# An attention pair with a mixture of experts on one core: a new prologue, routing work reordered, split last out-projections, and shared and routed expert pairs two units later

## The chip, the cores and the metric

One core of a Trainium2 chip runs the whole program. Its engines work side by side and are tied together by semaphores only: TensorE (PE; its weight loads are listed as PEld), VectorE (DVE), ScalarE (ACT), GpSimd (POOL), and the DMA queues, most of them fed by SyncE (SP), some by ACT and POOL. Each engine carries out its own list of instructions in order. The metric is the time of one execution on the device in microseconds (us).

## What is computed

The input x is 2 sequences of 512 tokens with 256 features, float32. All the rest is float32 too.

```python
x = L0_attn_x
xn = _layernorm(x, axis=-1)
x = x + _L0_attn_ref(xn, ...) + _L0_ffn_ref(xn, ...)
return x
```

`_L0_attn_ref` is causal attention with 16 heads of 128, biases on queries, keys, values and output. `_L0_ffn_ref` is a whole transformer block:

```python
x = rmsnorm(hidden_states, ln1_w)
q = (x @ wq) ...; k = (x @ wk) ...; v = (x @ wv) ...   # 16 query heads, 4 key/value heads
q = q * cos + rotate_half(q) * sin                      # k alike
attn = softmax(causal(q k^T / sqrt(D)))
x = resid + (attn v) @ wo
xn = rmsnorm(x, ln2_w)
probs = softmax(xn @ gate_w.T)                          # 32 experts
_, sel = top_k(probs + bias_e, 4)
rw = probs[sel]; rw = rw / max(sum(rw), 1e-12)
moe_y = sum over the 4 chosen experts of rw * ((silu(xn @ weg) * (xn @ weu)) @ wed)
shared = silu(xn @ wsg) * (xn @ wsu) @ wsd
return x + moe_y + shared
```

## The kernel before

The work is cut into 64 units of one head and one sequence each: units 0 to 31 (`HALF`) are the heads of the rotary attention inside the block, units 32 to 63 those of the plain attention. Every engine runs `step(n)` for n from -2 to 63 (`windows`, line 425), and in step n it works on several units at once: PE makes the scores of unit n+1, turns the probabilities of unit n, multiplies them with the values (`attend`), projects queries, keys and values of unit n+2 (`project`), and does half an output projection of an earlier pair of heads (`out_project`). The probabilities go around all engines: scores on PE, mask and row maximum on DVE (L1368), exponential on ACT (L1103), reciprocal of the sum on DVE (L1374), scaling on POOL (L675), transposes on PE (L955), and a split into a rounded part (ACT, L1118) and a rest (DVE, L1383). Matrix products of float32 data are made of three passes over such parts (`mm3`, L820). Below, "step n" is the stretch from the first scores product of unit n+1 (L940) to that of unit n+2.

What stands in `step` is written out by hand, and so is the order of the projections' results in the four PSUM banks j0, j1, zb and ob (`ring_of`, `CHUNK`, `BANK`). A bank is filled again only when the engine that empties it has said so (`kept`, `vacant`).

The prologue loads x (L443), then biases and norm weights, then the first weights, all on the SP queue. DVE takes mean and variance of each token tile of 128 (`bn_stats`, L1319), POOL raises to the power -1/2 (`power`, L602), DVE writes the normalised rows xn (L1329), ACT squares and sums them (L1081), DVE and POOL make the second factor, and DVE writes the rows xr of the inner root-mean-square norm (L1338). PE transposes xr and xn (`turn_xr`, `turn_xn`, L801), ACT and DVE split the result (L1094, L1354, L1092, L1352). POOL splits the weights (`weights`, L661 and L665). `b_O` is added on POOL in steps 1 and 2 (L767).

Between steps 34 and 40 the routing is done beside the attention: squares (SQUARED), rows scaled (SCALED), transposes T2, the logits L in step 36 (`LOGITS`, L874), then DVE's long list `route_0` to `route_3`: softmax, the four best of 32 (L1670, L1744), combine weights `cw` (L1725, L1755), ranks by a triangular product R in step 38 (`RANKS`, L881, L883), slot numbers (L1731), the match of slots and experts over 128x1024 elements (L1765, L1685, L1700). In the plain half, `route_1` stands before the queries and keys of the step are taken out of PSUM (`chunk`), `route_2` between them and the values' product `z_part`. POOL scatters the rows into `x_slots` in HBM (L686, 32 transfers, `SENT`: steps 40 to 43), SP then loads them in slots (L540) and loads the weights of the experts (L528, L531).

Four shared pairs of token tiles follow, one a step, in steps 40 to 43 (`DENSE` = HALF + 8), and 32 pairs of expert blocks, two a step, in steps 44 to 59 (`MOE` = HALF + 12): PE transposes X (L890), makes gate and up G (L902, L909) and down Y (L917). POOL adds the result to one of two sums in HBM by a scatter with addition (L711), in the step after. When both sums are complete, SP loads each in one transfer of 1 MB (L571), DVE adds those of the second sequence in step 63 (L1710), POOL those of the first (L781), DVE adds the last out-projections of steps 64 and 65 (L1470), and SP stores four pairs of tiles in order (L579).

The lines around the last steps on PE:

```python
windows(pe, step)
for n in (UNITS, UNITS + 1):
    out_project(n, 0, None)
    out_project(n, 1, None)
```

## Time and profile before

| | |
|---|---|
| median of 3 runs | 793.09 us (790.8 to 795.21) |
| the profiled execution's own time | 791.5 us |
| its span (first to last instruction) | 789.7 us |
| busy PE / DVE / ACT / POOL | 738.3 / 548.8 / 490.2 / 477.8 us |
| PE's share in the chain that ended last | 64% |
| mean granted clock of TensorE | 0.988 |
| read from and written to HBM | 51.75 MB, 24.82 MB |

The page gives each engine's busy time, then the span in 40 slices (a digit is the busy share in tenths; PEclk is TensorE's granted clock). A timeline row is: start, duration, engine, line, operation, output<-inputs, count, and in brackets the idle time of the engine before it with what ended it. Ends of matmuls are modelled, so a busy PE says less than the start of the next group.

### The profile page before, as it was taken

The numbers are of one execution on the slowest core, as the hardware profiler recorded it, in microseconds if no ns is written. First come the engines' busy times: TensorE is split into PE (matmuls) and PEld (weight loads), VectorE is DVE, ScalarE is ACT, GpSimd is POOL, SyncE is SP. The second block draws the span as 40 slices with busy tenths as digits, with TensorE's granted clock in tenths as the row PEclk, the third lists the DMA queues.
The fourth block names the chain that finished last, engine by engine and source line by source line (L and its number), as shares of the span: only waits on it lengthen the run. The fifth ranks groups of instructions, "written<-read, shape, count | busy, mean of one in ns | idle before, by whom it ended". The sixth has DMA issues, their size and how long they took to land.

```text
span 789.7 us, 14401 instructions
## 1 busy us (share of the span) xinstructions
PE 738.3 (93%) x4629; PEld 661.2 (84%) x4629; DVE 548.8 (69%) x1689; ACT 490.2 (62%) x1230; POOL 477.8 (60%) x552
## 2 busy tenths in 40 slices
PE   1899999999999999999988995999999999999995
PEld 1678888888888888989877885999999999999995
DVE  5878888797878887675788763555555655555575
ACT  3777768777777775666434662556655566555652
POOL 3679676776867684327223774566556675665543
PEclk9999999999999999999999997999999999999999
DMA  5000000100010099201000534566797677776351
GB/s 170 27 15 28 14 15 15 34 15 21 24 45 28 14 308 295 73 14 42 14 28 14 184 110 130 128 142 157 165 266 159 162 163 162 176 173 142 68 133 54
DMA packets 103491, 77.51 MB, mean 98 GB/s; under 512 B 6950, under 2 KB 102266, under 8 KB 103418
## 3 DMA queue, kind: packets, MB, share of 16 engines
q1 hardware_dynamic: 92234, 63.19, 28.1%
q0 software_dynamic: 10752, 12.74, 9.7%
q8 instruction: 38, 0.62, 0.4%
q10 hardware_dynamic: 432, 0.67, 0.3%
q14 instruction: 35, 0.29, 0.1%
HBM read 51.75 MB, written 24.82 MB: 97 GB/s over the span
## 4 chain that ended last, share of the span: by engine, by line
PE 64%; DVE 13%; ACT 9%; POOL 7%; issue 4%; DMA 2%; DVEq 0%; SPq 0%; POOLq 0%; ACTq 0%
PE j L820 17%; PE zb L820 8%; PE ob L820 8%; PE s L820 8%; PE t L955 6%; ACT probs L1103 4%; POOL x_slots_dram L686 4%; PE j L909 4%; DVE probsT L1383 3%; PE zb L909 2%; PE ob L909 2%; PE j L917 2%; ACT rope_swapped L1143 2%; ACT rope_swapped L1144 2%; DVE rope_sum L1415 1%
## 5 line engine op out<-in xcount | busy, mean ns | idle before, releaser
L675 POOL TENSOR_SCALAR probs<-probs,inv_sum 128x128 f32<-128x128 f32 x244 | 141.8, 592 | 166.9 <-DVE inv_sum L1374 162.9
L1103 ACT ACTIVATE probs<-probs,neg_max 128x128 f32<-128x128 f32 (+3 forms) x256 | 143.1, 560 | 126.4 <-DVE neg_max L1368 124.9
L820 PE MATMUL s<-k_heads,q_heads 128*128 128x256 f32 (+2 forms) x576 | 138.1, 360 | 3.4 <-DVE neg_max L1368 2.8
L1368 DVE CUSTOM_DVE_ANT_0 probs<-s,mask 128x128 f32<-128x128 f32 (+3 forms) x256 | 119.9, 484 | 11.7 <-PE s L820 6.6
L711 POOL DMA_INDIRECT moe_sum_dram<-late,slot_tokens x64 | 101.4, 1584 | 38.7 <-ACT late L1188 25.7
L1383 DVE TENSOR_TENSOR probsT<-t,probsT 128x384 fp32r<-128x384 f32 (+2 forms) x192 | 101.1, 547 | 12.7 <-ACT probsT L1118 11.9
L1118 ACT ACTIVATE probsT<-t 128x384 fp32r<-128x384 f32 (+2 forms) x192 | 89.8, 486 | 19.4 <-PE t L955 19.3
L955 PE MATMUL t<-ident,probs 128*128 128x128 f32 x640 | 94.3, 274 | 7.8 <-POOL probs L675 6.5
L820 PEld LDWEIGHTS s<-k_heads,q_heads 128*128 128x128 f32 x576 | 90.9, 189 | 10.2 <-DVE neg_max L1368 6.6
L955 PEld LDWEIGHTS t<-ident,probs 128*128 128x128 f32 x640 | 74.9, 140 | 16.6 <-POOL probs L675 8.6
L820 PE MATMUL zb<-probsT,v_heads 128*128 128x512 f32 (+2 forms) x351 | 68.3, 339 | 1.4 <-DVE probsT L1383 0.9
L820 PEld LDWEIGHTS zb<-probsT,v_heads 128*128 128x128 f32 x351 | 60.1, 189 | 8.2 <-DVE probsT L1383 1.4
L720 POOL TENSOR_TENSOR rope_swapped<-rope_swapped,rope 128x512 f32<-128x512 f32 x32 | 41.4, 1295 | 34.1 <-ACT rope_swapped L1144 34.1
L1374 DVE RECIPROCAL inv_sum<-row_sum 128x1 f32<-128x1 f32 x256 | 36.0, 156 | 34.0 <-ACT probs L1103 33.8
L820 PE MATMUL ob<-w_o,zT 128*128 128x256 f32 x420 | 58.4, 283 | 0.0
L820 PEld LDWEIGHTS ob<-w_o,zT 128*128 128x128 f32 x420 | 55.5, 190 | 2.6
L820 PE MATMUL j<-xrT,w_qk 128*128 128x512 f32 x192 | 53.1, 412 | 0.8 <-DVE rope_sum L1415 0.7
L1103 ACT ACTIVATION_READ_ACCUMULATOR probs<-probs,neg_max 128x1 f32 x256 | 47.9, 187 | 0.0
L726 POOL TENSOR_TENSOR q_heads<-rope_sum,q_heads 128x384 fp32r<-128x384 f32 x32 | 38.8, 1212 | 12.5 <-ACT q_heads L1211 10.7
L820 PE MATMUL j<-xnT,w_qk 128*128 128x512 f32 x174 | 45.5, 404 | 0.0
L820 PEld LDWEIGHTS j<-xrT,w_qk 128*128 128x128 f32 x192 | 34.3, 192 | 7.7 <-DVE rope_sum L1415 1.1
L820 PEld LDWEIGHTS j<-xnT,w_qk 128*128 128x128 f32 x174 | 32.8, 193 | 6.8
(251 smaller groups left out, 1576.9 us busy)
## 6 DMA issues: line engine op xcount, KB each, us to landing
x_slots_dram<-mask SPq DMA_DIRECT2D x1, 8480.0 KB, 38.3
late<-x_slots_dram SPq DMA_DIRECT2D x32, 265.0 KB, 4.5
late<-in_L_ffn_weg_dram SPq DMA_DIRECT2D x64, 128.0 KB
late<-in_L_ffn_weu_dram SPq DMA_DIRECT2D x64, 128.0 KB
late<-in_L_ffn_wed_dram SPq DMA_DIRECT2D x64, 128.0 KB
moe_sum_dram<-mask SPq DMA_DIRECT2D x2, 1152.0 KB, 8.8
raw_qk<-in_L_ffn_wq_dram SPq DMA_DIRECT2D x16, 128.0 KB, 2.2
raw_o<-in_L_ffn_wo_dram SPq DMA_DIRECT2D x8, 256.0 KB, 2.6
```

The lines of the kernel that those rows point to most:

```text
L675: pool.tensor_scalar(piece, piece, rinv[:, u % 2, i:i + 1], 1.0, ALU.mult, ALU.mult).then_inc(p_norm, 1)
L711: pool.indirect_dma_start(out=moe_sum[j][:, :], out_offset=bass.IndirectOffsetOnAxis(ap=ids[:, r % 4, j:j + 1], axis=0), in_=yb[:, r % 2, ...
L720: pool.tensor_tensor(swapped[kind], swapped[kind], sinT, ALU.mult).then_inc(rp_sin[kind], 1)
L726: pool.tensor_tensor(qT[:, v % 2, 1], rot_sum((kind, v))[:, P:S], qT[:, v % 2, 0].bitcast(f32), ALU.subtract).then_inc(rp_lo[kind], 1)
L820: m = pe.matmul(dst, lhs(a), rhs(b), start=first and i == 0, stop=last_ and i == 2, skip_group_check=skip)
L909: m = pe.matmul(dst[:, (2 * w + j) * P:(2 * w + j + 1) * P], wgu[(r - SHARED) % 3][:, j, k, w * P:(w + 1) * P], xbT[:, r % 2, k, j * P:(j ...
L955: m = pe.transpose(bT[at % 2][:, (j - lo_) * P:(j - lo_ + 1) * P], pr[:, u % 2, P_OFF[qt] + kt * P:P_OFF[qt] + (kt + 1) * P], ident[:, :])
L1103: act.activation(piece, piece, ACT.Exp, bias=nmax[:, u % 2, i:i + 1], scale=-1.0, accum_out=rsum[:, u % 2, i:i + 1]).then_inc(e_done, 1)
L1118: act.activation(pT[:, 0, (first - 1) * P:(b - 1) * P], bT[(3 * u + c) % 2][:, (first - a) * P:(b - a) * P], ACT.Copy).then_inc(pt_hi, 1)
L1368: ve.tensor_tensor_reduce(pr[:, u % 2, P_OFF[i]:P_OFF[i] + width], bS[i % 2][:, 0:width], mask_t[:, S - width:S], INV_SCALE, BIG, ALU.add, ...
L1374: ve.reciprocal(rinv[:, u % 2, i:i + 1], rsum[:, u % 2, i:i + 1]).then_inc(r_done, 1)
L1383: ve.tensor_tensor(pT[:, 1, cs], bT[(3 * u + c) % 2][:, (first - a) * P:(b - a) * P], pT[:, 0, cs].bitcast(f32), ALU.subtract).then_inc(pt ...
```

## The change

The program computes the same result. What it does:

- **Prologue.** xr is made straight from x with one factor, (var (1 + 1e-6) + 1e-11)^-0.5, which holds both norms; the squares and the first pass of xn fall away. Rows of the second sequence are made on POOL (`second_rows`). x of the second sequence is loaded behind the first weights; the small rows go on ACT's queue, ahead of the rotary table. ACT loads its table by an exponential of its own. PE makes six products into an unused bank (`keep_busy`).
- **xn** is written by POOL in steps 0, 1, 4 and 5 and transposed in a new chunk `XN` at the start of the step behind each; `b_O` is added in steps 9 and 17.
- **Rotary steps.** The values `Vx` are taken out of PSUM by DVE later in the step, and the last mask of the step comes before the probabilities' rest.
- **Routing.** `route_1` and `route_2` stand behind queries, keys and z. `cw` is gone: weights are normalised after the match, over 4 values. POOL makes the triangle and the ones (step 36) and the product of match and probabilities (`choice`, step 39).
- **Pairs.** DENSE = HALF + 10 and MOE = HALF + 14: shared pairs in steps 42 to 45, expert pairs in steps 46 to 61.
- **End.** The last out-projections are split by head; PE adds the experts' sums of the second sequence by products with the identity (`add_experts`) in place of DVE; SP loads the sums in four transfers, the second sequence first. Step 63's out-projection moves into step 62.

```diff
-    DENSE, MOE = HALF + 8, HALF + 12
+    DENSE, MOE = HALF + 10, HALF + 14
...
-    ACT_NORMS = (HALF + 9, HALF + 10, HALF + 11)
+    ACT_NORMS = (HALF + 8, HALF + 9, HALF + 10, HALF + 11)
...
-            for j in range(2):
-                sp.wait_ge(y_out[j], 16 * (PAIRS - SHARED))
-                sp.dma_start(macc[j], moe_sum[j][P:P + B * S, :].rearrange("(t p) d -> p t d", p=P)).then_inc(acc_in, 16)
+            for b in reversed(range(B)):
+                for j in range(2):
+                    sp.wait_ge(y_out[j], 16 * (PAIRS - SHARED))
+                    sp.dma_start(macc[j][:, b * TB:(b + 1) * TB, :],
+                                 moe_sum[j][P + b * S:P + (b + 1) * S, :].rearrange("(t p) d -> p t d", p=P)
+                                 ).then_inc(acc_in[b], 16)
...
+            def choice(n):
+
+                if n == RANKS + 1:
+                    pool.wait_ge(chosen_done, 1)
+                    pool.tensor_tensor(match, match, route[:, 0, :, 0:E].unsqueeze(2).to_broadcast([P, NT, TOPK, E]),
+                                       ALU.mult).then_inc(weighed, 1)
...
-                    if n == -2 and job[0] == "Q2":
+                    if n == -2 and job[0] == "Q3":
+                        first_powers(1)
                         q_sin(n, it)
+                        second_rows(range(TB, TB + 2))
                         q_lo(n, it)
+                        second_rows(range(TB + 2, NT))
                     weights(job, it)
+                choice(n)
...
-                if n in (1, 2):
+                    normal_power()
+                normal_rows(n)
+                if n in (GS + 1, 2 * GS + 1):
                     pool.wait_ge(bc_in, 32)
+                    pool.wait_ge(normal, NT)
...
+            def keep_busy(count):
+
+                for _ in range(count):
+                    pe.matmul(bT[0][:, :], ident[:, :], mask_t[:, :], start=True, stop=True)
...
+            def add_experts(n):
+
+                o = n - 2
+                half, b = o % 2, o % GS // 4
+                pe.wait_ge(acc_in[b], 32)
+                for t in range(2):
+                    for j in range(2):
+                        pe.matmul(bR[BANK["O", n]][:, t * D:(t + 1) * D], ident[:, :], macc[j][:, b * TB + 2 * half + t, :],
+                                  start=False, stop=False, skip_group_check=True)
...
+            def last_unit():
+
+                for t in range(2):
+                    out_project(UNITS, t, None, (0,))
+                turn_probs(UNITS - 1, 2, None)
+                for t in range(2):
+                    out_project(UNITS + 1, t, None, (0,))
+                attend(UNITS - 1, None)
+                for n in (UNITS, UNITS + 1):
+                    add_experts(n)
+                for n in (UNITS, UNITS + 1):
+                    for t in range(2):
+                        out_project(n, t, None, (1,))
...
+                did(ve.tensor_scalar(var[:, 1, ts], mv[:, ts, 1], 1.0 + 1e-06, 1e-11, ALU.mult, ALU.add), "var", b)
...
                 v_last = behind(n, 1, "Vx")
-                for ch in v_last:
-                    chunk(ch, it)
...
+                if v_last:
+                    mask_scores(n + 1, 3, it)
                 probs_lo(n, 2, it)
-                mask_scores(n + 1, 3, it)
+                if not v_last:
+                    mask_scores(n + 1, 3, it)
...
                 rope_sum(chs[0], it)
+                for ch in v_last:
+                    chunk(ch, it)
...
+                    for ch in chs[:2]:
+                        chunk(ch, it)
+                    z_part(n, it)
                     route_1(n)
-                    for ch in chs[:1]:
-                        chunk(ch, it)
-                    for ch in chs[1:2]:
-                        chunk(ch, it)
                     route_2(n)
-                    z_part(n, it)
...
                 if n == RANKS + 2:
-                    then(ve.tensor_tensor(match, match, cw.unsqueeze(2).to_broadcast([P, NT, TOPK, E]), ALU.mult))
+                    ve.wait_ge(weighed, 1)
+                    then(ve.tensor_reduce(x2r[:, :, D + 1 + TOPK:ROW], match, AX.X, ALU.add))
+                    then(ve.tensor_reduce(rsm[:, 3], x2r[:, :, D + 1 + TOPK:ROW], AX.X, ALU.add))
+                    then(ve.tensor_scalar(rsm[:, 0], rsm[:, 3], 1e-12, None, ALU.max))
+                    then(ve.reciprocal(rsm[:, 1], rsm[:, 0]))
+                    ve.tensor_tensor(x2r[:, :, D + 1 + TOPK:ROW], x2r[:, :, D + 1 + TOPK:ROW],
+                                     rsm[:, 1].unsqueeze(2).to_broadcast([P, NT, TOPK]), ALU.mult).then_inc(rows_done, 1)
```

## Rows read from the trace of the kernel before

**Rows 1.** Timeline of the prologue, from the first statistics to unit 1's scores.

```profile
5.97 1.40 DVE L1319 BATCH_NORM_STATS2 ln_stats<-acc_b 128x6 f32<-128x256 f32 x4 [5.97 <-DMA acc_b<-in_L_attn_x_dram]
...
8.01 1.04 POOL L602 TENSOR_TENSOR rstd<-var,minus_half 128x4 f32<-128x4 f32 x1 [5.48 <-DVE var L1325]
...
15.37 1.14 DVE L1338 TENSOR_SCALAR probs<-acc_a,rstd 128x256 f32<-128x256 f32 x4 [1.13 <-POOL rstd L602]
...
18.84 2.90 PE L820 MATMUL j<-xrT,w_kv 128*128 128x512 f32 x6 [0.94 <-DVE xrT L1354]
...
24.12 1.54 PE L820 MATMUL j<-xrT,w_kv 128*128 128x512 f32 x6
...
37.32 0.39 PE L940 MATMUL s<-k_first,rope_sum 128*128 128x128 f32 x2
```

**Rows 2.** Timeline: PE's wait for unit 1's first mask.

```profile
39.54 1.50 PE L820 MATMUL s<-k_heads,q_heads 128*128 128x384 f32 x6 [1.25 <-DVE neg_max L1368]
```

**Rows 3.** Timeline: b_O's second addition; PE's wait in step 7.

```profile
65.86 2.40 POOL L767 TENSOR_TENSOR acc_b<-acc_b,b_o 128x1024 f32<-128x1024 f32 x1
...
106.90 1.09 PE L955 MATMUL t<-ident,probs 128*128 128x128 f32 x8 [0.53 <-POOL probs L675]
```

**Rows 4.** Timeline of step 38: `cw` on DVE beside POOL's split, ranks on PE.

```profile
393.15 1.33 POOL L665 TENSOR_TENSOR w_qk<-raw_qk,w_qk 128x512 fp32r<-128x512 f32 x1
...
393.37 1.39 DVE L1725 TENSOR_TENSOR combine<-router 128x256 f32<-128x256 f32 x1
...
397.35 0.67 PE L881 MATMUL ob<-router,late 128*128 128x256 f32 x2 [2.10 <-DVE late L1750]
```

**Rows 5.** Timeline of step 40: waits, a shared pair's products, DVE's reduction.

```profile
421.17 0.46 PE L940 MATMUL s<-k_first,q_first 128*128 128x128 f32 x2 [1.10 <-DVE k_heads L1422]
...
425.98 0.79 PE L820 MATMUL s<-k_heads,q_heads 128*128 128x384 f32 x3 [0.97 <-DVE neg_max L1368]
...
426.61 1.89 PE L902 MATMUL ob<-late 128*128 128x256 f32 x8
...
432.10 1.20 DVE L1700 TENSOR_REDUCE late<-late 128x32 f32<-128x1024 f32 x1
```

**Rows 6.** Windows by step: length, busy us, clock, DMA share, GB/s.

```profile
363.07:380.97 17.90, 17.90 (x104) 16.09 (x103) 9.03 (x27) 8.25 (x22) 7.40 (x8) 0.81 0.16 44
421.17:435.56 14.39, 13.33 (x75) 11.52 (x75) 12.63 (x41) 5.76 (x16) 3.00 (x5) 1.00 0.08 19
474.07:501.44 27.37, 18.59 (x113) 16.68 (x112) 9.97 (x33) 10.15 (x25) 11.66 (x13) 0.81 0.31 94
501.44:517.89 16.45, 16.45 (x113) 15.08 (x111) 9.77 (x32) 9.87 (x26) 10.40 (x11) 1.00 0.70 162
748.20:758.43 10.23, 10.23 (x64) 9.25 (x63) 6.36 (x21) 6.21 (x17) 8.21 (x8) 1.00 0.44 63
...
767.49:789.70 22.21, 13.91 (x95) 12.14 (x93) 14.08 (x31) 6.36 (x17) 7.61 (x8) 0.97 0.14 48
```

**Rows 7.** Timeline: last row scattered, first transpose of an expert pair.

```profile
478.14 0.96 POOL L686 DMA_INDIRECT x_slots_dram<-late,dest  x1 [0.30 <-issue]
...
483.60 1.09 PE L890 MATMUL j<-ident,late 128*128 128x128 f32 x4 [8.78 <-DMA late<-x_slots_dram]
```

**Rows 8.** Timeline of the end: last scatter of a sum, last additions.

```profile
756.07 1.58 POOL L711 DMA_INDIRECT moe_sum_dram<-late,slot_tokens  x1 [0.16 <-issue]
...
774.89 5.59 POOL L781 TENSOR_TENSOR acc_b<-acc_b,late 128x512 f32<-128x512 f32 x4
...
786.44 0.69 DVE L1470 TENSOR_TENSOR acc_b<-ob,acc_b 128x512 f32<-128x512 f32 x1 [0.74 <-PE ob L820]
```

**Rows 9.** DMA view: KB of one, median us to landing.

```profile
late<-moe_sum_dram SPq DMA_DIRECT2D x2, 1024.0 KB, 5.7
...
moe_sum_dram<-late,slot_tokens POOLq DMA_INDIRECT x64, 5.1
out_dram<-acc_b SPq DMA_DIRECT2D x4, 256.0 KB, 2.1
```

More of the change, by code:

```diff
@@ L57, in attention_pair_moe_kernel @@
     BIG = 3.0e38
+    XN_UNITS = (0, 1, 4, 5)
     def chunks_of(n):
@@ L484, in _ @@
             kinds = ("KV", "Q0", "Q1", "Q2", "Q3", "O0", "O1")
-            for which in kinds:
+            load("KV", 0, 0)
+            sp.dma_start(accB[:, TB:2 * TB, :], xv[:, TB:2 * TB, :]).then_inc(x_in[1], 16)
+            for which in kinds[1:]:
                 load(which, 0, 0)
@@ L610, in _ @@
             pool.wait_ge(consts, 3)
-            for b in range(B):
-                power(0, b)
+            first_powers(0)
             def weights(job, it):
@@ L770, in _ @@
             weights(("KV", 0), None)
-            for b in range(B):
-                power(1, b)
             pool.wait_ge(rope_in, 16)
             windows(pool, step)
-            pool.wait_ge(acc_in, 32)
+            pool.wait_ge(acc_in[0], 32)
             kept(pool, ("O", UNITS - GS + 5))
```

272 lines of the change are left out of this document (138 added, 134 removed).

## The prediction

> **What bounds the kernel now.** I read the page first: PE is busy for 93% of the span and heads the chain that ended last, so what counts is where PE stands still or runs at half clock, and what is added to it. Next came the view of who waited for whom, for PE alone. Its largest entries are the start, where PE has nothing to do until constants and xr are there, and one wait of 8.78 us for the first expert rows [rows 7]; the rest are dozens of small ones. Then the windows, cut at each step's first scores product, and the timeline where a step is longer than its like. A plain step of the second half lasts 10.23 us with PE never idle, one with two expert pairs 16.45 [rows 6]. The surplus lies in four places, and the change touches all four: the prologue, 37.32 us long [rows 1]; the routing steps 36 to 40; step 44, 27.37 us instead of 16.45; and the end, 22.21 us from the start of step 62 [rows 6].
>
> **Prologue.** Before, the power for the first sequence is done at 8.01 + 1.04 = 9.05, and xr starts at 15.37 [rows 1], after xn, the squares and a second power. The new factor needs the first power only: 6.3 us go, less some 0.5 for four rows with two operations in place of one. x of the first sequence is in at 5.97, beside a rotary table and a second half of x; both now come later. A transfer of 512 KB lies between the rows for 256 KB (2.1 us) and 1024 KB (5.7 us) [rows 9], about 3.3 us by line, so up to 1.9 us are free; bounds 0 to 1.9, I take 1.3. The first six 512-column products take 2.90 us and a later group 1.54 [rows 1]: half clock and full. The six products of `keep_busy` fill PE's idle time before them; gain 0 (clock not granted in time) to 1.4, or a loss of about 1 if they are still running when xr is there. I take 0.8, since PE had nothing before that and works nearly without pause now. Rows of the second sequence move to POOL, ahead of the third and fourth query weights; its queue then holds power, sine product, two rows, query rest, two rows. By the old distances this lands where the old order did, seven small operations against two splits moved ahead. The xn transposes and four pairs of evictions leave the stretch, worth 2 us of PE, ACT and DVE before unit 1's scores. Sum: 6.3 - 0.5 + 1.3 + 0.8 + 2.0 = 9.9 us, bounds 6 to 12.
>
> **Rotary steps.** Unit 1's first mask waited for xn on DVE, 1.25 us at PE [rows 2]: -1.1. The xn work comes back as four chunks of four transposes (0.45 us), an ACT copy and a DVE rest of 0.7 us each, in steps 1, 2, 5 and 6, where PE is full: +0.6 each, +2.4. In step 5 the chunk shares bank ob with an out-projection that comes early on PE, which must wait for DVE: +0.7. The two b_O additions take 2.40 us of POOL each [rows 3]; before, the second stands ahead of the sine product of step 3, on which queries and scaling wait; of its length POOL could have hidden about 1 us, so 1.4 are on the path. In steps 9 and 17 POOL has more room, since no new keys or values are worked on beside it: 0 to 0.7 each, I take 0.3. Net -0.8. The later `Vx` brings the step's last mask, exponential and scaling 0.6 us forward; PE waits 0.53 us for that scaling in step 7 [rows 3] and in six more of the kind. Gain 0 to 0.53 each, I take 0.43: -3.0. Sum: -1.1 + 2.4 + 0.7 - 0.8 - 3.0 = -1.8.
>
> **Routing.** The key wait of 1.10 us in step 39 [rows 5] goes, with the ranks' wait of 2.10 [rows 4], since triangle and ones are POOL's by then and DVE's cw work (1.39 us [rows 4] and small instructions behind it) is gone. Following DVE's list through, I get steps 36 and 37 together unchanged (z no longer has routing work in its own wait), step 38 2.2 us and step 39 1.2 us shorter. Step 40 gives it back. There DVE now waits for POOL's product over 128x1024 elements, 2.40 us by the b_O row of that size [rows 3], where DVE did it itself in about the 1.20 that its reduction of that size takes [rows 5]. The product starts when DVE's match is done, and DVE has under 2 us of work to hide it. That reduction and four small ones stood later in the step, and now stand at once behind the wait. Queued behind them: the values' eviction, two reciprocals, the accumulation, and the masks of unit 41's last two tiles, on which its probabilities and PE wait. I count 3 us from match to the end of the wait and 2.1 for the sums, so step 40 takes about 15.6 us although the shared pair, 2.6 us, has left it: 14.39 - 2.6 = 11.8 [rows 6], +3.8. Sum: -2.2 - 1.2 + 3.8 = +0.4, bounds -3 to +3.
>
> In this trace DVE's product for cw took 1.39 us while POOL's split ran from 393.15 for 1.33 us, and ended when that ended [rows 4]. The Trainium skill (SBUF — State Buffer, "Who interferes with whom") has the rule: DVE and GpSimd share a pair of ports, and an instruction of DVE with two SBUF inputs, or in a two-port mode, is blocked for the whole length of a GpSimd instruction that has the pair. That rule speaks against this change. By it the small instructions behind the match could wait for POOL's product, and step 40 would be some 1.5 us longer.
>
> **Pairs two units later.** The last of 32 rows is scattered at 478.14 and PE gets its first expert rows at 483.60 [rows 8]. With MOE at step 46, two plain steps of 10.23 us stand before the four shared ones, and DVE hands over the rows some 7 us sooner, so the first X comes over 12 us after its rows. POOL needs 32 x 1.26 us for them (0.96 and 0.30 idle [rows 7]) and starts in step 40. The wait goes, and with it the half clock behind it (granted 0.81 in that step): 27.37 - 16.45 = 10.9 us [rows 6]. The two plain steps and the two pair steps trade places, which costs PE nothing. Gain 10.9, bounds 8 to 11.
>
> **End.** Before, the last scatter is issued at 756.07 [rows 8], two steps ahead, and the sums are in SBUF long before they are needed. Now the last scatter falls into step 62, by step 60's pattern 756.07 - 748.20 = 7.9 us after its start. It lands some 4.7 later, a little under the median of 5.1 [rows 9], as less runs beside it: 12.6. Then 0.5 MB for the second sequence is still to load, 3.3 us: 15.9, and 1 MB more for the first, 4.7 us by the slope (5.7 - 2.1) / 768 KB: 20.6. PE's part: eight float32 products of 256 columns; four of a shared pair are listed with 1.89 us, modelled end included [rows 5], so 3.1 to 3.8. With 1.5 for the second heads, 0.7 for an accumulation [rows 8] and 2.1 for a store [rows 9]: 24. POOL's part: four additions, 5.59 us with DVE beside them [rows 8], 5.2 alone: 25.8, then stores issued in order behind it: 29.2. The end was at 22.21 [rows 6]; +7.0, bounds +2 (both waits short) to +11 (a landing 1.5 us later and loads half as long again). What the split out-projections save DVE and PE, 2 us, is hidden behind this.
>
> **Sum.** -9.9 - 1.8 + 0.4 - 10.9 + 7.0 = -15.2 us against the profiled execution, 791.5 us: 776.3. That execution lies 1.6 us under the median of 793.09, so the median comes to 778; I say 777.
>
> One thing stays open: in step 36 the clock is 0.81 [rows 6], which is 17.90 x 0.19 = 3.4 us of PE lost; the small logits products stand just before the fall. It may come at another time or not at all; I keep it, and put 3.4 us in the bounds.
>
> **Rivals.** (A) The forecast, 777: 0.60. (B) The end hides better: PE takes the experts' rows at once and POOL's loads overlap, so the end grows by 2 us, and the clock stays up in step 36: 777 - 5 - 3.4 = 769. For it: sums of 1 MB loaded in 5.7 us before with nothing beside; against it: four POOL additions in a row. 0.17. (C) The prologue gains only the 6 us of the removed detour, and DVE's small instructions in step 40 end only with POOL's product, as DVE's did with POOL's in [rows 4], its 2.4 us and some wait behind: 777 + 3.9 + 3 = 784. 0.15. This is the result that the rule cited above would give. (D) The change doesn't do what it says, the wait for the first expert rows only moves, because POOL scatters later: 777 + 10.9 = 788. Against it: 32 x 1.26 = 40 us from step 40's beginning end before step 44 begins. 0.05. (E) Slower than before: in steps 40 and 41, now without shared pairs and with 5 us of waits, PE falls to half clock (1.2 GHz) and stays there for both plain steps, 2 x 10.23 = 20.5 us more: 777 + 20.5 = 797.5. It decides from the point at which waits in step 40 stretch so far that the granted clock falls, and it costs more than the whole gain only if it holds beyond one and a half steps. Against it: the fall in step 44 came after 8.78 us without work and was over within that step [rows 6, 7]. 0.03.
>
> **Numbers.** The range has to hold A with its bounds, most of B and of C: 766 to 787. A measurement of this kernel can tell about 0.5% (4 us) from no change: faster than 789.1 holds A, B, C but for their edges: 0.91; within 0.5%, to 797.1, D: 0.06; slower, E: 0.03.
>
> **What would show it.** Unit 1's scores at 27.4 us instead of 37.32; the first six 512-column products in under 2 us; no wait at the transposes of step 7 and its like; the ranks' products without wait; in step 40 a DVE wait on POOL and PE idle for 4 to 5 us; no wait at the first X, no half clock near it, and the X rows loaded 12 us ahead; in the end PE's first identity product about 16 us and POOL's first addition about 20.6 us after step 62's start, the last store 29. Wrong would be: a prologue held by const rows that come late on ACT's queue, an end that is hidden, or a fall of the clock in a place where there was none.

## The result, and the profile after

The changed kernel takes 804.2 us (median of 4 runs, 803.08 to 808.48), the kernel before 793.65 beside it. The two medians stand 1.3% apart; the ratio on record is 1.016, 95% interval 1.0135 to 1.0185. The change made the kernel slower. The forecast was 777 us, with 766 to 787 as its range. Its profiled execution has a span of 801.3 us against 789.7: 11.6 us more, where the forecast had 15.2 less.

Cut at the same marks as before (the first scores product of a unit, L996 now), the span divides as follows. The sum of the last column is the 11.6 us.

| stretch | before, us | after, us | difference | forecast |
|---|---|---|---|---|
| start to unit 1's scores | 37.32 | 31.76 | -5.6 | -9.9 |
| steps 0 to 7 | 71.91 | 93.77 | **+21.9** | -1.8 for steps 0 to 27 |
| steps 8 to 27 | 174.64 | 173.43 | -1.2 | |
| steps 28 to 35 | 79.21 | 79.18 | 0.0 | 0 |
| steps 36 to 40 | 72.49 | 69.86 | -2.6 | -2.2, since a shared pair of 2.6 moves out |
| steps 41 to 61 | 331.93 | 324.14 | -7.8 | -8.3, with that pair back |
| step 62 to the end | 22.20 | 29.14 | +6.9 | +7.0 |

The forecast and the two spans differ by 26.8 us. Steps 0 to 27 make 22.5 of them, nearly all in the first eight steps, and the prologue 4.3; the routing, the pairs and the end are within 0.5 us each. The windows of steps 0, 1, 2, 3, 4 and 5 of the changed kernel (length, busy time and count of PE, PE's weight loads, DVE, ACT and POOL, then the granted clock, DMA share, GB/s):

```profile
31.76:46.54 14.78, 9.84 (x49) 7.76 (x49) 6.99 (x22) 7.28 (x18) 10.58 (x11) 0.93 0.07 20
46.54:60.80 14.26, 10.48 (x49) 8.60 (x48) 7.62 (x22) 8.00 (x19) 6.82 (x8) 0.86 0.00 0
60.80:69.71 8.91, 8.61 (x55) 7.69 (x54) 7.84 (x24) 6.91 (x17) 6.35 (x8) 0.96 0.01 2
69.71:77.65 7.94, 7.94 (x51) 7.10 (x50) 7.02 (x23) 5.98 (x15) 7.35 (x10) 1.00 0.12 33
77.65:91.76 14.11, 10.87 (x61) 9.49 (x60) 6.90 (x21) 6.61 (x16) 9.37 (x12) 0.90 0.10 30
91.76:108.79 17.03, 11.35 (x62) 9.79 (x60) 8.23 (x23) 8.12 (x19) 8.33 (x10) 0.90 0.03 8
```

Steps 0, 1, 4 and 5 are five to eight us longer than in the kernel before (9.72, 9.28, 8.93 and 9.28 there), PE is busy for 67 to 77% of them, and the clock is below 1 in each. The view of who PE waited for (total us, times, longest) names the cause:

```profile
PE ob L901 <- POOL acc_a L621: 14.9, 4, 4.6
PE s L870 <- DVE neg_max L1446: 7.0, 5, 4.0
PE j L1037 <- DMA late<-moe_sum_dram: 3.5, 1, 3.5
...
PE s L996 <- POOL q_heads L768: 2.6, 1, 2.6
```

L901 is the transpose of xn in the new chunk `XN`, L621 the row that `normal_rows` writes. The largest entry of before, 8.78 us for the first expert rows [rows 7], is gone; 14.9 us in four waits stand in its place. In the timeline of PE the wait ends at 43.74, and the six 512-column products behind it take 2.59 us where a group without a wait takes 1.63:

```profile
37.29 1.63 PE L870 MATMUL j<-xrT,w_kv 128*128 128x512 f32 x6
38.77 1.03 PE L1011 MATMUL t<-ident,probs 128*128 128x128 f32 x8
43.74 0.66 PE L901 MATMUL ob<-ident,acc_a 128*128 128x128 f32 x4 [3.94 <-POOL acc_a L621]
44.15 2.59 PE L870 MATMUL j<-xrT,w_qk 128*128 128x512 f32 x6
46.54 0.63 PE L996 MATMUL s<-k_first,rope_sum 128*128 128x128 f32 x2
```

The same stretch on POOL: two splits of weights, then the two rows, which end at 43.68, and then 4.37 us without work:

```profile
39.30 0.62 POOL L686 TENSOR_SCALAR w_o<-raw_o 128x512 fp32r<-128x512 f32 x1
40.00 1.27 POOL L690 TENSOR_TENSOR w_o<-raw_o,w_o 128x512 fp32r<-128x512 f32 x1
41.26 2.42 POOL L621 TENSOR_SCALAR acc_a<-acc_b,ln_mean_var,rstd 128x256 f32<-128x256 f32 x2
48.06 1.30 POOL L762 TENSOR_TENSOR rope_swapped<-rope_swapped,rope 128x512 f32<-128x512 f32 x1 [4.37 <-ACT rope_swapped L1227]
```

So the engines wait for one another in a ring. PE has turned unit 1's probabilities and is free, but `XN` stands ahead of unit 3's query projection and of unit 2's scores in its list, and those two feed everybody else. POOL makes the rows last in its step. DVE has ended its last work at 41.28 and ACT at 40.43; neither has anything to do until the rows are there, and afterwards POOL waits for what PE could have delivered 4 us earlier.

The prologue's timeline, where rows 1 showed 5.97, 15.37, 18.84 and 37.32:

```profile
4.80 1.40 DVE L1405 BATCH_NORM_STATS2 ln_stats<-acc_b 128x6 f32<-128x256 f32 x4 [4.80 <-DMA acc_b<-in_L_attn_x_dram]
...
7.93 2.58 DVE L1416 TENSOR_SCALAR probs<-acc_b,ln_mean_var,rstd 128x256 f32<-128x256 f32 x4 [1.17 <-POOL rstd L601]
...
13.04 1.63 PE L870 MATMUL j<-xrT,w_kv 128*128 128x512 f32 x6 [0.51 <-DVE xrT L1431]
...
23.43 0.46 PE L996 MATMUL s<-k_first,rope_sum 128*128 128x128 f32 x2 [2.63 <-POOL q_heads L768]
...
31.76 0.46 PE L996 MATMUL s<-k_first,rope_sum 128*128 128x128 f32 x2
```

And the end, to be read against rows 8: the last scatter in step 62, PE's wait for the sums, POOL's additions, the stores.

```profile
779.49 1.58 POOL L753 DMA_INDIRECT moe_sum_dram<-late,slot_tokens  x1 [0.16 <-issue]
...
788.82 5.29 PE L1037 MATMUL j<-late,ident 128*128 128x256 f32 x16 [3.45 <-DMA late<-moe_sum_dram]
...
791.75 5.08 POOL L829 TENSOR_TENSOR acc_b<-acc_b,late 128x512 f32<-128x512 f32 x4 [10.68 <-DMA late<-moe_sum_dram]
...
795.65 2.65 SPq L578 DMA_DIRECT2D out_dram<-acc_b  x4
```

### The profile page after: what moved, and what is told of

Its sections match the earlier page's. It is cut to its first block, busy times and chain, and to the rows that moved or that the text cites. A ratio compares the mean times of both kernels' runs of the same rounds, so it can differ in the third digit from the quotient of the medians.

```text
span 801.3 us, 14430 instructions
## 1 busy us (share of the span) xinstructions
PE 753.5 (94%) x4657; PEld 669.8 (84%) x4657; DVE 539.6 (67%) x1667; ACT 490.4 (61%) x1219; POOL 494.2 (62%) x564
## 4 chain that ended last, share of the span: by engine, by line
PE 69%; DVE 9%; POOL 7%; ACT 7%; DMA 3%; issue 2%; SPq 2%; ACTq 0%; POOLq 0%; DVEq 0%
PE j L870 19%; PE zb L870 9%; PE ob L870 9%; PE s L870 9%; PE t L1011 6%; PE j L965 3%; ACT probs L1186 3%; PE ob L965 2%; POOL probs L700 2%; DVE probsT L1461 2%; PE zb L965 2%; PE j L973 2%; DVE probs L1446 1%; PE s L996 1%; DVE rope_sum L1493 1%
## 5 line engine op out<-in xcount | busy, mean ns | idle before, releaser
L870 PE MATMUL s<-k_heads,q_heads 128*128 128x256 f32 (+2 forms) x576 | 140.5, 365 | 7.4 <-DVE neg_max L1446 7.0
L870 PEld LDWEIGHTS s<-k_heads,q_heads 128*128 128x128 f32 x576 | 92.7, 193 | 13.9 <-DVE neg_max L1446 10.2
L870 PEld LDWEIGHTS zb<-probsT,v_heads 128*128 128x128 f32 x342 | 58.2, 188 | 8.1 <-DVE probsT L1461 0.9
L870 PE MATMUL j<-xrT,w_qk 128*128 128x512 f32 x192 | 57.0, 436 | 0.3 <-DVE rope_sum L1493 0.3
L870 PEld LDWEIGHTS j<-xrT,w_qk 128*128 128x128 f32 x192 | 36.7, 204 | 7.2 <-DVE rope_sum L1493 0.7
```

Source lines behind the costliest of these rows:

```text
L870: m = pe.matmul(dst, lhs(a), rhs(b), start=first and i == 0, stop=last_ and i == 2, skip_group_check=skip)
```

## The experiments

Every experiment was measured in one of three groups, with runs of the kernel before beside it; their medians were 793.13, 792.93 and 793.13 us. A time from a single run has no interval; what such an experiment shows is read from its trace.

**1. XN one step later.** Only the place of the chunk `XN` changes, that is PE's four transposes and the two evictions behind them; POOL's work stays where it is.

```diff
-    XN_UNITS = (0, 1, 4, 5)
+    XN_UNITS, ROWS_AT = (1, 2, 5, 6), (0, 1, 4, 5)
...
-                if n in XN_UNITS:
-                    p = XN_UNITS.index(n)
+                if n in ROWS_AT:
+                    p = ROWS_AT.index(n)
```

> The changed kernel with one thing different: TensorE turns each pair of xn tiles one step later than it does now (XN in steps 2, 3, 6 and 7), while GpSimd makes the rows where it makes them now (steps 0, 1, 4, 5). All work is the same. My theory: what the changed kernel lost is TensorE's in-order wait for these rows at XN (14.9 us in four waits in its trace), the half clock behind each wait and the restart of the chain of scores; then the four waits are gone, steps 0 to 7 last about 74 us instead of 93.8, and the time is 783 to 787 us. Rival 1, XN's own work (eight transposes, two evictions, the bank ob that it shares): the loss stays, 797 us or more, with the idle time now in front of other products. Rival 2, GpSimd's two rows of 1.2 us each as such, which push back the rotation and the scaling of the next step: about half of the loss stays, 790 to 796 us.

Measured: 784.32 us, 0.9891 of before (0.9863 to 0.9919). Steps 0 to 7 take 72.94 us, 20.8 less than in the changed kernel, and no transpose of xn waits, as the theory had it. Timeline of PE, the first `XN` and what follows:

```profile
48.94 0.60 PE L901 MATMUL ob<-ident,acc_a 128*128 128x128 f32 x4
...
50.77 0.38 PE L996 MATMUL s<-k_first,rope_sum 128*128 128x128 f32 x2
```

This settles the main question. The work of `XN`, POOL's rows and the shared bank are all still there and cost 1.0 us over the 71.91 of before. What cost 20.8 us was the place of one chunk in PE's list: 14.9 us of waits, and 5.9 for the half clock behind them (2.59 us instead of 1.63 for the group of six products above) and for what the stopped chain costs. No run separates these two.

**2. The rows ahead of the weights.** This leaves `XN` in its bad place and changes the length of the wait alone.

```diff
                 send_rows(n)
+                normal_rows(n)
                 for job in jobs_of(n)[1 if n == -2 else len(first_jobs):]:
...
-                normal_rows(n)
```

> The changed kernel, XN where it puts it, but GpSimd makes the rows of xn ahead of the weights of the same step instead of behind them. The weights take 1.9 us of GpSimd in step 0, nothing in step 1, 1.2 us in steps 4 and 5. My theory: TensorE's waits at XN shrink by just these times, 3.9, 3.1, 3.2 and 4.6 us to about 2.0, 3.1, 2.1 and 3.4, and steps 0 to 7 last about 89.5 us instead of 93.8. Rival, what costs is the chain of scores started late and the half clock, whatever the length of the wait: steps 0 to 7 stay within 1 us of 93.8. Rival, the weights are now too late for the next queries: a new wait for them.

Measured: 800.46 us in its one run. The four waits are 1.97, 3.11, 2.05 and 3.32 us, where the theory had 2.0, 3.1, 2.1 and 3.4. PE's waits (total, times, longest):

```profile
PE ob L901 <- POOL acc_a L621: 10.4, 4, 3.3
```

Steps 0 to 7 last 89.51 us, 4.3 less than in the changed kernel, and the waits are 4.5 us shorter. In sum the length of POOL's list in front of the rows passes into the time. Step by step it does so only roughly, since the clock fell at other places: step 4 is 2.5 us shorter for 1.2 us less wait, with a granted clock of 1.00 behind the wait of 2.05 us, and step 1 is 0.3 us longer with the same wait.

**3. Pairs two units later, on the kernel before.**

```diff
-    DENSE, MOE = HALF + 8, HALF + 12
+    DENSE, MOE = HALF + 10, HALF + 14
...
-    ACT_NORMS = (HALF + 9, HALF + 10, HALF + 11)
+    ACT_NORMS = (HALF + 8, HALF + 9, HALF + 10, HALF + 11)
```

> The kernel before with the shared and expert pairs two units later and nothing else of the change. My theory: the wait of 8.8 us at the first X and the half clock behind it go (steps 44 and 45 together -10.9 us), and the end, which still loads each sum in one transfer of 1 MB, adds on VectorE and GpSimd and stores after that, grows by at least as much: the last scatter starts 7 us into step 62, two loads of 5.7 us and the additions of 5.6 us follow, 33 to 35 us instead of 22.2. So 793 to 797 us, the gain of the middle paid back at the end. Rival, the end is hidden as well as the changed kernel's (29.1 us): 789 to 791 us. Rival, the move gains only the wait: 796 to 800 us.

Measured: 795.56 us, 1.0038 of before (1.0016 to 1.0059), as the theory had it. The wait at the first X, 8.78 us before, is gone, and the end, 22.2 before, is now 34.8 us long. In it PE stands behind DVE, which adds the experts' sums in one block before it takes out the last values:

```profile
779.16 5.70 DVE L1710 TENSOR_TENSOR acc_b<-acc_b,late 128x512 f32<-128x512 f32 x4 [9.24 <-DMA late<-moe_sum_dram]
...
785.57 2.93 PE L820 MATMUL j<-w_o,zT 128*128 128x256 f32 x12 [13.51 <-DVE zT L1396]
```

The move alone gains in the middle and gives more than all of it back at the end. The split end of the change (29.1 us) saves 5.6 of these 12.6 us.

**4. Pairs one unit later, and as before, with XN mended.** On the kernel of experiment 1:

```diff
-    DENSE, MOE = HALF + 10, HALF + 14
+    DENSE, MOE = HALF + 9, HALF + 13
```

> As the kernel with XN one step later, and shared and expert pairs one unit later than before instead of two (steps 41 to 44 and 45 to 60). My theory: in the changed kernel the first rows of the slots landed at 493.5 us and step 45 begins at 497, so there is no wait at the first X; the last scatter is complete a step earlier, so TensorE doesn't wait for the sums (3.5 us) and doesn't add them at the half clock (5.3 us for 16 products, which should be about 2.7): the tail from step 62 on falls from 29.1 to 22 to 24 us and the time is 776 to 780 us. Rival: the rows land relative to the steps as late as before, a wait of 2 to 4 us with a half clock comes back at the first X, and nothing is gained over the kernel with XN one step later: 783 to 788 us.

> As the kernel with XN one step later (784.3 us), but with the shared and expert pairs where they stand before the change (steps 40 to 43 and 44 to 59), all other parts of the change kept. With one unit later it took 775.7 us. My theory: the scatters end and the first rows land at the same moment as there (475.2 us), but TensorE wants them at 468.2 us, in step 44: a wait of 7 us comes back with the half clock behind it, and the end stays at 22 us, since the sums were complete in time there already. So 784 to 788 us, and one unit later is the best of the three places. Rival, the scatters come earlier too because fewer steps lie before them, and the wait is under 3 us: 776 to 781 us.

Measured: one unit later 775.69 us, 0.9789 (0.9759 to 0.9819); as before (HALF + 8, HALF + 12) 777.32 us, 0.9803 (0.9769 to 0.9837); two units later, experiment 1, 784.32 us. With one unit later the theory holds (it had 776 to 780 us): the transposes find their rows and sums, and the end takes 21.95 us. Timeline of POOL, SP and PE: last row scattered, first rows loaded, first X, the identity products of the end without a wait:

```profile
467.08 0.96 POOL L711 DMA_INDIRECT x_slots_dram<-late,dest  x1 [0.31 <-issue]
470.47 1.00 SPq L536 DMA_DIRECT2D late<-x_slots_dram  x2
481.04 0.60 PE L946 MATMUL j<-ident,late 128*128 128x128 f32 x4
...
765.81 3.62 PE L1037 MATMUL j<-late,ident 128*128 128x256 f32 x16
```

The second of these expectations was wrong, and its rival right. With the pairs unmoved the wait at the first X of step 44 is only 2.17 us (the view of waits has 1.5 us for another X as well), without a half clock:

```profile
472.22 0.63 PE L946 MATMUL j<-ident,late 128*128 128x128 f32 x4 [2.17 <-DMA late<-x_slots_dram]
```

Step 44 takes 18.80 us here, 27.37 in the kernel before [rows 6], 16.45 without a wait. So 8.6 of the 10.9 us are gone with the pairs unmoved. The last row is scattered at 466.60, 2.7 us ahead of step 44's start, where rows 7 had 4.1 behind it (478.14 against 474.07). Of these 6.8 us, 2.4 are rows handed over sooner (the first scatter stands 11.1 us behind step 40's start instead of 13.5), and 4.4 are step 40 itself, which takes 18.83 us with a shared pair in it, 14.39 before [rows 6]: time lost there that the wait gives back. Moving the pairs buys 2.4 us in this kernel whether by one unit or by two, and the second unit costs 7.4 at the end (29.4 against 22.0). The lead of one unit over none, 1.6 us by the medians, is within the intervals.

**5. The product of match and probabilities.** Three kernels take the delay in step 40 apart. First, on the changed kernel, the product back on DVE:

```diff
+                    ve.wait_ge(chosen_done, 1)
+                    ve.tensor_tensor(match, match, route[:, 0, :, 0:E].unsqueeze(2).to_broadcast([P, NT, TOPK, E]),
+                                     ALU.mult).then_inc(weighed, 1)
```

> The changed kernel with the product of match and probabilities (128x1024) on VectorE, right behind the comparison, instead of on GpSimd. My theory: GpSimd's product of 2.34 us holds up VectorE's copy of 128x32 (1.98 us instead of 0.17), so VectorE gains 1.8 us and pays 1.2 us for the product: the copy falls back to 0.2 us, TensorE's wait in step 40 stays near 3.4 to 4.0 us and step 40 stays within 1 us of 16.28 us. Rival, the product on GpSimd is worth its place (it takes 1.2 us off VectorE and the copy was slow for another reason): the copy stays slow and step 40 grows to over 17.3 us.

Measured: 804.0 us in its one run; step 40 takes 15.73 us instead of 16.28, with a granted clock of 1.00 in it instead of 0.90. In the changed kernel (timeline of POOL and DVE) the first copy behind the product's start takes 1.98 us:

```profile
436.59 2.34 POOL L728 TENSOR_TENSOR late<-late,router 128x1024 f32<-128x1024 f32 x1 [4.37 <-DVE late L1826]
...
436.99 1.98 DVE L1832 COPY late<-router_small 128x32 f32<-128x32 f32 x1
439.00 0.17 DVE L1833 COPY late<-slot_numbers 128x8 f32<-128x8 f32 x1
```

With the product on DVE it takes 0.17 us, although DVE pays 1.23 for the product:

```profile
437.75 1.23 DVE L1827 TENSOR_TENSOR late<-late,router 128x1024 f32<-128x1024 f32 x1
...
439.45 0.17 DVE L1832 COPY late<-router_small 128x32 f32<-128x32 f32 x1
```

Second, on the kernel of one unit later, the copies written as products by 1.0:

```diff
-                    then(ve.tensor_copy(x2r[:, :, D + 1:D + 1 + TOPK], top8[:, :, 0:TOPK]))
+                    then(ve.tensor_scalar(x2r[:, :, D + 1:D + 1 + TOPK], top8[:, :, 0:TOPK], 1.0, None, ALU.mult))
```

> The kernel at 775.7 us (XN one step later, pairs one unit later), its two small copies in step 39 still on VectorE and behind the start of GpSimd's product, but written as a multiplication by 1.0 instead of a copy. With copies the first took 1.98 us and ended with GpSimd's product. My theory: what is held up is the copy's form, not every VectorE work from SBUF to SBUF beside GpSimd, since a comparison and a sum of 128x32 ran in 0.2 us beside the same product: the first takes about 0.2 us, the masks begin at once, and step 40 falls from 16.3 to 16.8 us to under 15.9 us, as it did with the copies on GpSimd. Rival, any VectorE work that reads and writes SBUF is held up: it takes 1.9 us again, step 40 stays at 16.3 or more.

Measured: 774.18 us in its one run, and my theory fell: the product by 1.0 is held up just as long, step 40 takes 16.91 us. But a sum of 128x32 elements, begun while the same product ran, is not:

```profile
415.05 2.34 POOL L728 TENSOR_TENSOR late<-late,router 128x1024 f32<-128x1024 f32 x1 [4.38 <-DVE late L1826]
...
415.16 0.18 DVE L1830 TENSOR_REDUCE block_expert<-late 128x1 f32<-128x32 f32 x1
...
415.45 1.98 DVE L1832 TENSOR_SCALAR late<-router_small 128x32 f32<-128x32 f32 x1
```

Third, the copies moved to POOL, and two of the prologue's second rows moved to DVE:

```diff
+                    pool.tensor_copy(x2r[:, :, D + 1:D + 1 + TOPK], top8[:, :, 0:TOPK]).then_inc(weighed, 1)
+                    pool.tensor_copy(x2r[:, :, D], slot_t[:, 1:1 + NT]).then_inc(weighed, 1)
...
-                        second_rows(range(TB, TB + 2))
                         q_lo(n, it)
-                        second_rows(range(TB + 2, NT))
+                        second_rows(range(TB, TB + 2))
```

> The kernel at 775.7 us (XN one step later, pairs one unit later) with two more edits. Prologue: of the four second rows two go to VectorE (0.6 us each there, 1.2 on GpSimd), and GpSimd makes q_lo ahead of its two. Step 39: the two small copies behind the match go from VectorE to GpSimd, behind its product. My theory: TensorE's wait of 2.6 us for q_lo falls to about 1 us and GpSimd has 2.4 us less ahead of the scaling of unit 0, so unit 1's scores begin 1.5 to 2 us earlier; in step 40 the copy that stood 1.98 us is gone, the masks begin 2 us earlier, TensorE's wait of 4.0 us falls to about 2 us and the half clock behind it may go, so step 40 falls from 16.75 to 13.5 to 15 us. Time 770 to 773 us. Rival: it isn't the copy but any VectorE work on SBUF that is held up while GpSimd multiplies; then the mask stands the 2 us, step 40 doesn't change, and the time is 773.5 to 775 us.

Measured: 775.41 us, 0.9786 (0.9752 to 0.9819), no better than 775.69. That lies above the theory's 770 to 773 us and just above the rival's range. Step by step it is half a success. In the prologue PE's wait for the query rest falls from 2.63 to 1.00 us, but a wait of 2.57 us for unit 0's scaling (L701) follows, with a half clock behind it. Counted from x's arrival, unit 1's scores begin at 25.8 us (30.71 - 4.87) instead of 27.0 in the changed kernel. In step 40 the masks run at full speed beside POOL's product, and PE waits 1.76 us instead of 3.99:

```profile
414.50 2.38 POOL L730 TENSOR_TENSOR late<-late,router 128x1024 f32<-128x1024 f32 x1 [4.38 <-DVE late L1833]
...
414.89 0.28 DVE L1449 CUSTOM_DVE_ANT_0 probs<-s,mask 128x128 f32<-128x128 f32 x1
...
415.24 1.49 PE L873 MATMUL s<-k_heads,q_heads 128*128 128x384 f32 x6 [1.76 <-DVE neg_max L1449]
```

But DVE then waits 1.38 us for the product, the later masks come no earlier, PE waits 2.03 us at the step's last transposes, and steps 40 and 41 together take 29.93 us, against 29.59 with the copies in place.

**6. The rows spread, and the match later.** On top of this:

```diff
+    ROWS_AT = {0: (0, 1), 1: (2, 3), 2: (4,), 3: (5,), 4: (6,), 5: (7,)}
...
                     if nxt:
                         invert(n + 1, 3, it)
+                    weigh(n)
```

`weigh` holds the sums and the division of `route_0`; the comparison moves from `route_3` of step 39 behind the first two masks of step 40.

> The kernel above (rows split, copies on GpSimd) with two more edits. The rows of xn: two in step 0, two in step 1, then one a step in 2 to 5, instead of two in 0, 1, 4 and 5. Step 40: the comparison (1.2 us) stands behind the first two masks instead of ahead of them, and the sums and the division of the weights (2.0 us) behind the last mask instead of between the masks. My theory: step 6 (10.5 us, TensorE waits 1.8 us for GpSimd's scaling behind the rows) falls to about 9; in step 40 VectorE has the same work but the masks come 3 us earlier, so the step falls to 12 to 13.5 us; the first scatter starts up to 3 us later in the step, which the 6 us between the landing of the first rows and their use cover. 1.5 to 3 us faster than the kernel above, 768 to 771 us. Rival, VectorE is full in step 40 and what leaves the masks comes back at queries and keys: no more than 1 us faster. Rival, the rows land too late: a wait at the first X in step 45, slower than the kernel above.

Measured: 770.58 us, 0.9713 (0.9677 to 0.9749). Step 6 falls from 10.50 to 8.98 us, step 40 from 15.79 to 12.93, steps 40 and 41 together to 25.83. Steps 0 to 7 are now 71.81 us. The theory holds, and the gain of 4.8 us by the medians is larger than its 1.5 to 3.

**7. Without keep_busy.** On the kernel of one unit later, the six products of the prologue into an unused bank left out, on which no result depends.

> The kernel at 775.7 us without the six products into an unused bank in the prologue; the result doesn't depend on them. My theory: TensorE's clock is at its lower level at the first projections without them, six products take 2.9 us instead of 1.6 for at least the first two groups, and unit 1's scores begin 1 to 2.5 us later, counted from the moment that x has landed. Rival, the first projections wait for VectorE and GpSimd anyway and their cover is enough: less than 0.5 us later.

Measured: 775.52 us in its one run. The first projection groups take 2.90 and 2.26 us; with keep_busy, in the changed kernel, 1.63 and 1.55:

```profile
12.98 2.90 PE L867 MATMUL j<-xrT,w_kv 128*128 128x512 f32 x6 [0.95 <-DVE xrT L1428]
15.68 2.26 PE L867 MATMUL j<-xrT,w_qk 128*128 128x512 f32 x6
```

Counted from x's arrival, unit 1's scores begin at 28.1 us (33.03 - 4.94); with keep_busy 27.0 in the changed kernel (31.76 - 4.80) but 28.3 in the kernel of one unit later (33.22 - 4.90). There the first three filling products (two matmuls each) had ended sooner, at 6.52 instead of 7.42, so that PE waited 1.67 us for the rows of the gate instead of 0.97, although these came no later (8.19 against 8.38). Behind the longer wait the granted clock stood at 0.5, four matmuls of the filling took 3.64 us instead of 1.98, and the transposes of xr, behind them in PE's list, began at 12.10 instead of 10.63:

```profile
8.19 0.27 PE L845 MATMUL zb<-ident,const_rows 52*128 52x52 f32 x1 [1.67 <-DMA rope_swapped<-in_L_ffn_gate_w_dram]
...
8.63 3.64 PE L839 MATMUL t<-mask,ident 128*128 128x512 f32 x4
12.10 1.04 PE L860 MATMUL s<-ident,probs 128*128 128x128 f32 x8
```

In the kernel of experiment 5 with the product on DVE it was the same after a wait of 1.69 us. So the first half of the theory holds, the slow groups, and the second only in part: the filling gains about 1 us, or nothing where the clock falls in its midst, and the time is that of the kernel with it (775.69).

**8. Two more edits on the fastest.** Weights of the fourth query head later, the experts' sums of the end in two parts.

```diff
+                add_experts(UNITS)
                 attend(UNITS - 1, None)
-                for n in (UNITS, UNITS + 1):
-                    add_experts(n)
+                add_experts(UNITS + 1)
```

> The fastest kernel so far (770.6 us) with two more edits. Prologue: GpSimd splits the weights of the fourth query head (1.15 us) behind the scaling and the query rest of the last prologue step instead of ahead of them. End: TensorE adds the experts' sums for the first of its two banks ahead of the last unit's product with the values, where it had 0.4 us idle, and the rest behind it. My theory: GpSimd is what unit 0's turned probabilities wait for (2.7 us in front of them), so unit 1's scores begin 0.8 to 1.2 us earlier (30.8 to about 29.8); the end falls from 21.95 by 0.3 to 0.6 us, as TensorE's work stays the same. Time 768.5 to 770 us. Rival, VectorE's reciprocal of the last row sum is next in line and the prologue gains under 0.3 us; or the sums' first half delays the last unit's values by its whole 1.7 us and the end grows: 770.5 to 772 us.

Measured: 768.07 us, 0.9683 (0.966 to 0.9707): the fastest version, 25 us ahead of the kernel before and 36 ahead of the changed one. The stretch from unit 0's to unit 1's scores falls from 9.24 to 7.21 us, more than the theory had: PE's wait for the scaling falls from 2.68 to 1.36 us, and no half clock follows it. But PE's first projection began 2.1 us later in this execution (the rows of the gate came 1.1 us later, and a half clock followed the wait for them), so unit 1's scores stay at 30.84. The end is 21.88 us, 0.1 shorter: PE's gap was filled, and the path did not hang on it. The profiled execution has no half clock in steps 36 and 40; in the one of experiment 6 step 36 had lost 3.2 us to it, which is most of the 4.2 us between the two profiles.

## Why the prediction was wrong

**Rotary steps, the step that failed.** "The xn work comes back as four chunks ... in steps 1, 2, 5 and 6, where PE is full: +0.6 each" priced `XN` by its work and put the wait for its rows at nothing. The runs showed four waits, 14.9 us in all, and 20.8 us in steps 0 to 7 that go with them. The work was priced nearly right: with the transposes one step later, steps 0 to 27 are 0.1 us shorter than before (72.94 + 173.49 against 71.91 + 174.64), where the forecast had -1.8. With the rows spread as well they are 1.8 shorter (71.81 + 172.97), but that kernel places POOL's rows otherwise than the change does, so that the same figure comes out is luck. What the sentence left out is when the rows exist. I took rows made in one step and transposed in the next for a lead of a step. But `normal_rows` stands last in POOL's step, and `XN` first in PE's, ahead of the query projection. The row that shows it was on record: b_O's second addition, last in POOL's step 2, starts at 65.86 [rows 3], while the mark of PE's step 3 is at 64.68 (37.32 + 9.72 + 9.28 + 8.36). POOL's tail starts 1.2 us behind that mark, and two rows of 1.21 us would end 3.6 us behind it. `XN` stands even before the mark, ahead of a query projection that PE starts at 63.20 in the kernel before:

```profile
63.20 1.64 PE L820 MATMUL j<-xrT,w_qk 128*128 128x512 f32 x6
```

By these rows PE would wait for about 5 us (65.86 + 2.42 - 63.20, an estimate); the four waits were 3.1 to 4.6. I used the row of b_O for its duration, not for its place. I had also given the rows no price: 2.42 us on POOL for two. Experiment 6 shows part of it, with step 6 at 8.98 us instead of 10.50.

**Prologue: -5.6 for -9.9.** The terms one by one. x arrives 1.17 us sooner (1.3 forecast). From its arrival to xr's start 6.3 us go, as forecast. The four rows take 2.58 us instead of 1.14, 1.4 lost where I took 0.5 (single ones 0.49 to 0.90 us, while POOL splits weights beside them). The first six products gain 1.3 (0.8 forecast). So unit 0's K and Q stand about 7 us earlier, and at unit 0's scores 6.1 are left (29.52 to 23.43), at unit 1's 5.6. The failed sentence is "By the old distances this lands where the old order did": POOL's queue with sine product (1.76), two rows (3.02) and query rest holds unit 0's scores for 2.63 us, and the 2.0 us for the xn work that left never came out. Part of them is the clock: it stood at half behind that wait, and unit 0's other scores took 3.24 us instead of 2.20:

```profile
23.64 3.24 PE L870 MATMUL s<-k_heads,q_heads 128*128 128x256 f32 x9
```

Experiments 5 and 8 bear this out: with two rows on DVE the wait is 1.0 us, and with the fourth weights out of the way the stretch between the two units' scores is 7.2 us instead of 8.3. Rival C had this size of prologue.

**Routing: 0.0 for +0.4, by luck.** Steps 36 to 40 are 2.6 us shorter, which is just the pair that left. Step 38 gains 2.2 as forecast. Step 39 gains nothing (12.70 to 12.82), step 37 loses 0.7 (DVE reaches its first mask 4.8 us behind the step's start instead of 3.7, since the softmax work of step 36 now stands behind keys, queries and z; this is read from the two timelines, not tested), and step 40 takes 16.28 where I had 15.6, with a granted clock of 0.90. Against that step 36 gained 3.2 us since the clock didn't fall there in this execution; it does in others (experiment 1: 16.34 us, experiment 6: 17.89, against 14.74).

In step 40 DVE's copy was held to the end of POOL's product, 1.98 us instead of 0.17. So was a product by a constant, while the sum over 128x32 elements took 0.18 us and the masks, which read PSUM and SBUF, 0.28 beside POOL. The Trainium skill (SBUF — State Buffer, "Who interferes with whom") says that copies and `tensor_scalar` can take the pair of ports that DVE shares with GpSimd, that `tensor_reduce` never contends on trn2, and that the other side is blocked for the whole instruction. It also says that an instruction with one SBUF input at most, outside those modes, does not contend, which fits the masks. The traces agree in all of these, and since copy and `tensor_scalar` stand there side by side, my rewriting of the one as the other could not help. One `tensor_scalar` with one element per partition (L1831, 0.15 us) was not held; no run here tests why. The prediction read the same effect from [rows 4] a little too neatly: DVE's product for cw ended at 394.76, 0.3 us behind POOL's split (394.48), not with it.

**Pairs: -10.4 for -10.9, credited to the wrong part.** The wait and its half clock are gone, as forecast. Experiment 4 shows that with the other edits 8.6 us of it go without any move. "DVE hands over the rows some 7 us sooner" was too much: it was 2.4, and the longer step 40 did the rest. (The rows that the prediction cites there as rows 8 are rows 7.) And the prediction took the two units as given. One plain step is 10.23 us [rows 6], more than the whole wait of 8.78 [rows 7], so the rows on record already said that the second unit buys nothing, while the term for the end, +7.0, was its price.

**End: +6.9 for +7.0.** Last scatter 7.35 us after step 62's start (7.9 forecast), first identity product after 16.7 (16), POOL's first addition after 19.6 (20.6), the end after 29.1 (29.2). Of the forecast's last 3.4 us, from the additions' end to the last store's, only the 2.1 of a store have a row behind them; they measured 4.5 (24.7 to 29.1), and the additions, 1.0 us sooner than forecast, made up for it. The half clock there (5.29 us for 16 products, 3.62 without the wait) was not forecast.

**The rivals.** None was this one. The time lies where the prediction gave 0.03, slower than before. Rival E came nearest in kind: the clock fell where there had been no fall, which the prediction also names as a sign of being wrong, but it fell in the first eight steps, behind each wait for POOL's rows. No rival asked for each moved pair of producer and consumer whether it becomes a wait.

The terms measured make 11.6: -5.6 + 20.7 (steps 0 to 27) + 0.0 (36 to 40 with the pair's 2.6 added) - 10.4 (41 to 61 with it taken off) + 6.9.

## What to carry to other kernels

Price a moved step twice: by its work, and by its place, the time at which its input exists against the time at which the consuming engine reaches it, counted in each engine's own list. An operation at the end of one engine's step and one at the start of the next engine's step have no lead between them, and if the consumer feeds the producer again, the wait stops the ring: here 14.9 us of waits went with 20.8 us of time. When work is delayed to hide a wait, delay it by no more than the wait: the second unit here bought nothing and cost 7 us at the end.

## What the runs showed of the hardware

- POOL takes 1.21 us for 128x256 elements with a subtraction and a multiplication whose operands are both one value per row, and 0.43 us (L686) for the same size with two constants. DVE takes 2.58 us for four of the former and 1.44 for two (1.12 and 0.40), in both cases with POOL at work beside it.
- Waits of 2 to 4.6 us on PE were followed by a stretch at a granted clock of 0.5 in most cases, not in all: in experiment 4 a wait of 2.17 us had none, and in experiment 5 the wait of 3.44 us had none where one of 3.99 had. In the prologue waits of 1.53 to 1.69 us had one too. The Trainium skill (TensorE: Matmul & The Clock Gate, "What's actually happening") says that the same kernel may differ from run to run in how many of its first products run at the lower clock. The runs agree that a kernel differs from run to run, though they do not single out its first products: the four runs of the changed kernel had mean granted clocks of 0.973 to 0.984. Step 36 took 14.74, 16.34 and 17.89 us in three kernels that have the same work in it.
- A DVE instruction held up by POOL shows in the profile as busy, 1.98 us long, not as idle. The same copy without POOL's product beside it, at 0.17 us, gives it away.
